# A two-layer graph network: forty rows a group fetched one by one on SyncE

## What is computed

```python
h = relu(layernorm(x))
z = (h @ W).reshape(N, 8, 16)
e = leaky_relu(el[src] + er[dst])            # el, er: z times attention vectors
a = exp(e - emax[dst])
x = x + segment_sum(z[src] * a, dst) / segment_sum(a, dst) + bias

h = relu(layernorm(x))
s, v = h[:, :32] @ W_up_s, h[:, 32:] @ W_up_v
w = silu(silu(edge_f @ A1 + b1) @ A2 + b2) @ A3
x = x + map_out(segment_sum(products(s[src], v[src], edge_y, w), dst) / 10)
```

## Time and profile before

| | us |
|---|---|
| median of 3 runs | 4053.57 |
| lowest, highest | 4052.04, 4056.43 |
| the profiled execution | 4047.16 |
| its span, first to last instruction | 4045.0 |
| GpSimd busy | 2957.0 |
| TensorE busy | 2624.4 |
| VectorE busy | 2500.3 |

### The profile page before, as it was taken

The page is one execution under the profiler, slowest core; times in us unless marked ns, Lnnn a source line. Parts: engine busy times, 40 slices in busy tenths (PEclk is TensorE's granted clock), DMA queues, the critical chain, the costliest instruction groups (busy, mean ns, idle before and its releaser), DMA issues.

```text
span 4045.0 us, 45184 instructions
## 1 busy us (share of the span) xinstructions
PE 2624.4 (65%) x11198; PEld 1908.0 (47%) x11199; DVE 2500.3 (62%) x6079; ACT 1012.2 (25%) x1447; POOL 2957.0 (73%) x3136
## 2 busy tenths in 40 slices
PE   3545555545555555545468888787887878788787
PEld 2434444444444444444445555555555555555554
DVE  7444444444444444445367777777777878777777
ACT  4333333233333233323231111111111111111111
POOL 2777777777777777777757777777777777777775
PEclk8666666666666666666679999999999999999999
DMA  4222222222222222222212222222222222222221
GB/s 126 61 60 61 60 61 60 60 60 61 61 60 61 60 61 61 61 60 62 60 44 59 57 59 59 59 60 57 58 58 60 58 60 59 59 60 59 58 59 47
DMA packets 139545, 245.74 MB, mean 61 GB/s; under 512 B 53964, under 2 KB 85814, under 8 KB 139414
## 3 DMA queue, kind: packets, MB, share of 16 engines
q0 software_dynamic: 100032, 217.87, 22.2%
q1 hardware_dynamic: 39352, 26.89, 2.4%
q10 hardware_dynamic: 144, 0.80, 0.1%
HBM read 235.32 MB, written 10.03 MB: 61 GB/s over the span
## 4 chain that ended last, share of the span: by engine, by line
POOL 44%; issue 21%; PE 16%; DVE 9%; DMA 8%; ACT 1%; DVEq 1%; POOLq 0%; ACTq 0%; SPq 0%
POOL rows L436 44%; PE pair L1299 6%; PE pair L1225 5%; DMA rows<-up_tab,idx 5%; DMA rows<-z_tab,idx 3%; DVE share L966 2%; PE pair L1256 1%; DVE share L1074 1%; DVE share L1070 1%; PE pair L1246 1%; PE pair L1250 1%; DVE acc L869 1%; DVE share L1068 1%; PE pair L1270 1%; DVE share L1079 1%
## 5 line engine op out<-in xcount | busy, mean ns | idle before, releaser
L436 POOL DMA_INDIRECT rows<-z_tab,idx x1563 | 1480.8, 947 | 547.5 <-issue 515.2
L436 POOL DMA_INDIRECT rows<-up_tab,idx x1563 | 1474.8, 944 | 518.2 <-issue 458.9
L1225 PE MATMUL pair<-share,acc 128*128 128x136 f32 x3126 | 755.5, 433 | 828.3 <-DVE share L966 828.3
L1225 PEld LDWEIGHTS pair<-share,acc 128*128 128x128 f32 x3126 | 701.2, 326 | 960.6 <-DVE share L966 958.9
L1299 PE MATMUL pair<-share,acc 128*128 128x256 f32 x3126 | 810.7, 404 | 311.1 <-DVE share L1079 309.9
L1299 PEld LDWEIGHTS pair<-share,acc 128*128 128x128 f32 x3126 | 581.5, 196 | 693.4 <-DVE share L1079 596.9
L957 DVE TENSOR_TENSOR share<-rows,share 128x64 f32<-128x64 f32 x196 | 44.5, 227 | 883.7 <-DMA rows<-z_tab,idx 883.0
L1067 DVE TENSOR_TENSOR share<-rows,pair 128x384 f32<-128x384 f32 x391 | 216.7, 554 | 343.8 <-DMA rows<-up_tab,idx 333.4
L1256 PE MATMUL pair<-weights_sb,share 128*128 128x256 f32 x1576 | 393.6, 394 | 31.3 <-ACT acc L583 31.3
L570 ACT ACTIVATE share<-pair,front_sb 128x512 f32<-128x512 f32 x198 | 136.1, 688 | 1005.1 <-PE pair L1246 1005.1
L1256 PEld LDWEIGHTS pair<-weights_sb,share 128*128 128x128 f32 x1576 | 310.2, 199 | 86.3 <-issue 40.5
(11 more groups left out here) (167 smaller groups left out, 2395.0 us busy)
## 6 DMA issues: line engine op xcount, KB each, us to landing
rows<-z_tab,idx POOLq DMA_INDIRECT x1563, 2.6
rows<-up_tab,idx POOLq DMA_INDIRECT x1563, 2.5
ef_sb<-in_edge_f SPq DMA_DIRECT2D x50, 128.0 KB, 2.7
z_tab<-rows SPq DMA_DIRECT2D x7, 504.0 KB, 3.2
y_sb<-in_edge_y SPq DMA_DIRECT2D x50, 64.0 KB, 1.8
x_sb<-in_x SPq DMA_DIRECT2D x7, 448.0 KB, 6.9
up_tab<-acc SPq DMA_DIRECT2D x49, 64.0 KB, 1.6
out<-x_sb SPq DMA_DIRECT2D x48, 64.0 KB
```

What stands on the lines that cost most here:

```text
L436: pool.indirect_dma_start(out=rows[:, s, t, 0:width], out_offset=None, in_=table, in_offset=bass.IndirectOffsetOnAxis(ap=indices[:, t:t + ...
L1225: mm = t.matmul(bank[2 + h][:, 0:MW], hot[:, s, i, :], msg[:, h, i, :], start=(i == 0), stop=(i == tiles - 1))
```

## The change

In 48 of the 49 groups, in both layers, the gather of the last column of slot 3 covers partitions 0 to 87 alone. Partitions 88 to 127 of that column are filled by SyncE with 40 plain transfers of one row each, whose source row is a register value. The indices of these edges come as an input of their own (`src_single`, 48 x 40), loaded into one partition of the memory of `dst_rel` after that is last read (`columns_set`). SyncE loads 20 of them at a time into registers. Each transfer adds 16 to one semaphore for each layer, and VectorE waits for it ahead of slot 3 (layer 1) or of its second half (layer 2). SyncE begins a group's fetch when `msg1[3]` of the group before is set, so that the place is free. In layer 1 its stores of `up_tab` now stand between the fetches, by groups; it waits until all of them have landed before the first loads of layer 2. In layer 2 the fetch stands ahead of the group's other transfers.

```diff
+SINGLE = 40
+SG = P - SINGLE
...
+            def fetch_single(tab, width, group, fetched):
+
+                for c in range(0, SINGLE, 20):
+                    _, nodes = nc.values_load_multi_w_load_instructions(
+                        single_i[0:1, bass.ds(group * SINGLE + c, 20)], engines=(mybir.EngineType.SP,), min_val=0,
+                        max_val=NODES - 1, skip_runtime_bounds_check_because="they are sources, below NODES")
+                    for i, node in enumerate(nodes):
+                        at = SG + c + i
+                        sp.dma_start(rows[at:at + 1, U - 1, T - 1, 0:width], tab[bass.ds(node, 1), 0:width])\
+                          .then_inc(fetched, 16)
+
+            sp.wait_ge(G["columns_set"], 1)
+            sp.dma_start(single_i, src_single).then_inc(loads["single"], 16)
+            sp.wait_ge(s_in["stored_early"], 16 * REUSED)
+            sp.wait_ge(s_in["stored"], 16 * (BI - REUSED))
+            sp.wait_ge(loads["single"], 16)
             sp.wait_ge(G["ready_set"], 1)
-            with sp.Fori(0, NB) as b:
-                store_up(b)
+            with sp.Fori(0, passes1) as k:
+                with sp.Fori(0, GI - 1) as q:
+                    fetch_single(z_tab, ZW, q, s_l1["single"])
+                    blocks(sp, mybir.EngineType.SP, q + 1, store_up)
+                    hold(sp, s_l1["msg1"][U - 1], k * GI + (q + 1))
+                hold(sp, s_l1["msg1"][U - 1], k * GI + GI)
+            last_blocks(sp, store_up, GI)
+            sp.wait_ge(s_mid["stored"], 16 * NB)
...
-                    blocks(sp, mybir.EngineType.SP, q, store_block)
-                    if isinstance(r, int):
-                        return
+                    if isinstance(r, int):
+                        blocks(sp, mybir.EngineType.SP, q, store_block)
+                        return
+                    fetch_single(up_tab, HIDDEN, q, s_l2["single"])
+                    blocks(sp, mybir.EngineType.SP, q, store_block)
...
             def gather(s, indices, table, width, done, n=T):
                 for t in range(n):
-                    pool.indirect_dma_start(out=rows[:, s, t, 0:width], out_offset=None, in_=table,
-                                            in_offset=bass.IndirectOffsetOnAxis(ap=indices[:, t:t + 1], axis=0))\
+                    by = slice(0, SG) if n == T and s == U - 1 and t == T - 1 else slice(0, P)
+                    pool.indirect_dma_start(out=rows[by, s, t, 0:width], out_offset=None, in_=table,
+                                            in_offset=bass.IndirectOffsetOnAxis(ap=indices[by, t:t + 1], axis=0))\
                         .then_inc(done[t // HT], 16)
...
             set_columns()
+            dve.sem_inc(G["columns_set"], 1)
...
+                            if s == U - 1:
+                                dve.wait_ge(s_l1["single"], fetched)
...
+                            if s == U - 1 and hf == 1:
+                                dve.wait_ge(s_l2["single"], fetched)
```

More of the change, by code:

```diff
@@ L64, in bc, with gnn_kernel @@
     return wide.broadcast_to(shape)
-def gnn_kernel(nc, x, src, dst, dst_lin, edge_y, edge_f, bias, front, weights, out):
+def gnn_kernel(nc, x, src, src_single, dst, dst_lin, edge_y, edge_f, bias, front, weights, out):
     with ExitStack() as ctx:
@@ L136, in gnn_kernel @@
         assert PARTS_AT + 2 * GE <= 4 * COLS and (U + 1) * GE <= COLS
-        dst_rel = sb("dst_rel", [P, NG, T])
+        early = sb("early", [P, max(NG * T, (GI - 1) * SINGLE)])
+        dst_rel = early[:, 0:NG * T].rearrange("p (g t) -> p g t", t=T)
+        single_i = early[0:1, 0:(GI - 1) * SINGLE].bitcast(I32)
         win_f = sb("win_f", [P, NG])
@@ L237, in gnn_kernel @@
         loads = {n: sem(f"load_{n}") for n in
-                 ("x0", "x1", "front", "weights", "dst", "lin", "src", "bias", "win")}
+                 ("x0", "x1", "front", "weights", "dst", "lin", "src", "single", "bias", "win")}
         zeroed = sem("zeroed")
@@ L244, in gnn_kernel @@
             "pass_set", "out_w_ready", "up_w_ready", "lin_ready",
-            "sums_cleared", "ready_set", "cleared")}
+            "sums_cleared", "ready_set", "cleared", "columns_set")}
         def named(tag, names):
@@ L263, in gnn_kernel @@
         idx_set = sem("idx_set")
-        s_l1 = named("edges", ("open", "er_sum")) | slot_sems("edges", ("spread", "square", "turned", "er", "scored", "score",
+        s_l1 = named("edges", ("open", "er_sum", "single")) | slot_sems("edges", ("spread", "square", "turned", "er", "scored", "score",
                                                          "exp", "msg0", "msg1", "agg", "added", "rows0", "rows1"))
-        s_l2 = named("l2", ("h1", "h2", "tp", "first", "weighted", "dotted")) | slot_sems("l2", ("h1_act", "h2_act")) \
+        s_l2 = named("l2", ("h1", "h2", "tp", "first", "weighted", "dotted", "single")) | slot_sems("l2", ("h1_act", "h2_act")) \
             | {n: sems(f"l2_{n}_buf", 2) for n in ("y", "ef")}
@@ L288, in blocks, with last_blocks @@
             return hi
-        def last_blocks(eng, work):
-            lo = eng.value_load(ready[0:1, GI + 1:GI + 2], min_val=0, max_val=NB - 1)
+        def last_blocks(eng, work, at=GI + 1):
+            lo = eng.value_load(ready[0:1, at:at + 1], min_val=0, max_val=NB - 1)
             with eng.Fori(lo, NB) as b:
@@ L306, in gnn_kernel @@
                    "rows1": [GI * 16 * HT] * (U - 1) + [(GI - 1) * 16 * HT]}
+        FETCHED = 16 * SINGLE
         class Own:
@@ L410, in _ @@
                 hold(sp, s_l2["h1"], (k + 1) * (NG + AHEAD))
+                hold(sp, s_l1["msg1"][U - 1], (passes1 + k + 1) * GI)
                 hold(sp, s_l1["added"][U - 1], (passes1 + k + 1) * QUADS)
@@ L938, in four_tiles @@
                     landed = dve.snap(q * (16 * HT) + 16 * HT, min_val=16 * HT, max_val=GI * 16 * HT)
+                    fetched = dve.snap((k * (GI - 1) + q + 1) * FETCHED, min_val=FETCHED, max_val=PASSES1 * GI * FETCHED)
                     _, slots = nc.values_load_multi_w_load_instructions(
@@ L1345 @@
             .reshape(NG + U, P, T).transpose(1, 0, 2)),
+        "src_single": np.ascontiguousarray(
+            laid(src, 0, extra).reshape(GI, U, P, T)[:GI - 1, U - 1, SG:, T - 1]).reshape(1, (GI - 1) * SINGLE),
         "dst": np.ascontiguousarray(
```

## The result

The changed kernel takes 4058.57 us, the median of 20 runs, against 4052.58 us of the kernel before in as many runs beside it: a ratio of 1.0016, with a 95% interval of 1.001 to 1.0023. It is 0.16% slower. I had forecast 13 us less; it came out 6 us more. The profiled execution's span is 4052.2 us, 7.1 above the 4045.0 of before; both profiled executions are short ones of their kernels (4054.28 and 4047.16 us).

A forecast was written before the change was run, and what follows sets the result against it. The prediction took the pace of GpSimd's gathers to bound both layers. From the median of 4053.57 us, -14.2 for fewer rows and +1.2 at the turn of the layers, -13.0 together, gave 4040.6 us, range 4017 to 4059.

The forecast's parts named there:

- The bound: Both layers: the pace of GpSimd's gathers, 1.25 us each, sets the time, 3906 us of the 4045.
- The price of a row on GpSimd: Last gather of slot 3: 40 rows fewer save 0.148 us a gather, 14.2 us over 96 gathers.
- (a): Rival: a gather costs an instruction, 88 rows save under 0.097 us; time 4045.5 to 4054.8 us; chance 0.22.
- the first term: GpSimd's 96 gathers of 88 rows: -14.2 us in the sum.
- the turn: Between the layers: the first feature load leaves about 1.2 us later and GpSimd stands longer, +1.2 us once.
- (c): Rival: a gather of 88 rows is slower than one of 128, by 0.1 to 0.3 us; 4064 to 4084 us; chance 0.08.
- SyncE's fetch and its cover: SyncE's 40 transfers take 21.5 us a group, the loop closes at 27, 13 us below the pace; cost 0.
- Rival (b): SyncE becomes the pace from 0.84 us a row; at 0.90, +240 us, 4294 us; chance 0.12.

The follow-up runs named there:

- the sweep: Kernel before, no fetch by SyncE, ten gathers of a group cut to 16 to 120 rows, each followed by one of 128: 4045.66 us in one run.
- the last experiment: Against the kernel with 48 gathers fewer, SyncE's wait for stored up_tab moved behind its first loads of layer 2: 3989.56 us, ratio 0.9861 to the kernel before.
- the 32 rows: Changed kernel with 32 rows a group fetched by SyncE instead of 40 and a gather of 96: 4049.43 us, ratio 1.0013 to the kernel before.

## Why the prediction was wrong

**The bound.** Right. GpSimd's pace is the clock of both layers: 48 gathers less gave 55.6 us. One reading was too smooth: of the 59.3 us before TensorE's sums, 139 times 0.30 and the stall of 9.2 make only 50.6. The rest are three stalls of 4.0, 4.0 and 1.0 us in layer 2, each right behind a stretch (10.2, 10.2 and 3.4 us long) in which TensorE's granted clock reads 0.5. They are as large after the change, in sum.

**The price of a row on GpSimd.** This is the step that failed. I had a lower bound of nought and an upper one of 0.295 us for 40 rows and took the middle, 0.148 us, though the only rows that bore on it, equal times for 576 and 512 bytes and a fixed gap, spoke for the instruction; my own list had nothing against (a). The middle of two bounds was no estimate: by the slope of the sweep 40 rows are 40 x 0.74 ns = 0.03 us, a fifth of it, and nearly half of that is taken back in the next gather (0.013 us). And for 88 rows the sign is the other one. In place of -96 x 0.148 = -14.2 us stands +96 x 0.061 = +5.9 us. That 4058.57 still lies in the stated 4017 to 4059, by 0.4 us, is luck: the upper end was made of (a) and 4 us of scatter, with no gather dearer.

The sentence of the Trainium skill that I set against the gain, in "DMA: Bandwidth & Descriptors", section "Anatomy of one DMA", that many descriptors come before their cost is seen, agrees with the 0.74 ns a row. By it the first term would have been about nought, and the sum the +1.2 us of the turn.

**Rivals (a) and (c).** The ratio is within (a)'s 0.2%, or at its edge, but the time is 3.8 us above the 4054.8 at which (a) ended. (a)'s reason, a price of the instruction, is shown by the sweep and by the whole gather taken away. But the sign is (c)'s, a short gather that takes longer than a full one, at 0.061 us with its successor where I had priced it at 0.1 to 0.3. I gave (c) 0.08 because by the Trainium skill, "DMA: Bandwidth & Descriptors", section "Why a DMA increments its semaphore by 16 and not by 1", 88 rows would go to 11 engines with eight rows each, no more than now. What the trace shows to grow is GpSimd's own time in the instruction (the landing of these gathers it doesn't show), and there the counts that this rule deals to 16 engines (16 to 112 in steps of 16) are the cheap ones and those with a smaller divisor (120: 15, 88: 11, 100 and 40: 10) the dear ones. The rule finds the families; my conclusion from it was contradicted. That the engines' number is the cause isn't shown.

**SyncE's fetch and its cover.** Right. I had estimated 0.50 us a row and 21.5 us a group; it took 0.46 and 18.5, and the price of nothing held with 16 us to spare: VectorE never waits for these rows in the changed kernel, and the fetch alone lengthens neither the last gather of a group nor the next. Rival (b), from 0.84 us a row, had no part in it.

**The turn.** The mechanism was right, the size not: +0.57 us instead of +1.2. Relative to layer 2's first gather the feature load left 1.0 us later (1.36 us ahead of it instead of 2.36), and about half of that came through, as 1.03 us gave 0.5 in the last experiment. The trace shows what hides some of the rest: TensorE's first matmul on these features began 0.85 us later (1.21 us behind that gather instead of 0.36), but its granted clock rose from 0.5 to 1.0 nearly as early (14.0 us behind it, and 13.6 before the change), so that one fewer of the radial network's matmuls (line 1256 before, 1295 after) took 631 ns instead of 379. The sums then began 0.60 us later.

**What I had not in the sum.** 1.5 us of layer 1, in the first gather of slot 3. The 1.57 us by which the first gather starts earlier are no gain of the change: over all eight traces it starts between 71.9 and 73.4 us.

## What to carry to other kernels

Where an engine issues gathers at one pace whatever their bytes, the price is the instruction's: count instructions, not rows, and move work off that engine until a whole instruction goes. Between two far bounds take the end that the nearest rows speak for, and when a kind of instruction is to run in a size that the trace doesn't show, let the price be negative too. Keep row counts of a gather a multiple of 16, and see that the queue that takes over the rows ends well before they are read.

## What the runs showed of the hardware

A gather whose row count 16 doesn't divide costs GpSimd 0.04 to 0.08 us more than the line of the others, and any gather of under 128 rows lengthens the next one, by 0.013 us in one family and 0.033 in the other. Why the next one pays is open.

A transfer of one row with its address from a register costs SyncE 0.46 to 0.49 us, loads of registers included, in runs of 40 and of 64. Between 576 and 512 bytes there is no difference to see: forty take 18.55 and 18.51 us, the medians of layers 1 and 2.

The first gather of slot 3 in layer 1 takes 0.97 us instead of 0.94 wherever SyncE fetches beside it (the changed kernel, the fetch without the shorter gather, the 32 rows). With the short gather alone it is two gathers of slot 2, columns 6 and 7, that do (0.967 and 0.957 us), though SyncE fetches nothing. So it isn't SyncE's traffic alone. Timelines of GpSimd and of VectorE in the kernel after, at the same time, and then of both in the kernel before:

```profile
1068.91 0.98 POOL L468 DMA_INDIRECT rows<-z_tab,idx  x1 [0.30 <-issue]
```

```profile
1068.78 0.29 DVE L949 TENSOR_SCALAR share<-x_sb,share 128x128 f32 x1
1069.64 0.29 DVE L951 COPY share<-pair 128x128 f32<-128x128 f32 x1 [0.57 <-PE pair L1234]
```

```profile
1068.04 0.94 POOL L436 DMA_INDIRECT rows<-z_tab,idx  x1 [0.30 <-issue]
```

```profile
1068.25 0.29 DVE L916 TENSOR_SCALAR share<-x_sb,share 128x128 f32 x1
```

It goes with VectorE's work on a finished block of targets, which the edits move against the gathers. After the change the step of line 949 begins in GpSimd's 0.30 us between two gathers, 0.13 us ahead of the longer one; before (line 916) it begins 0.21 us inside a gather. The three kernels with the fetch have both cases, 47 blocks each. In 39, 33 and 38 the step begins in the gap, 0.11 to 0.13 us ahead of a gather, and every one of those gathers takes 0.97 to 0.99 us. In the other 8, 14 and 9, and in all 47 of the kernel before, it begins inside a gather, and that one takes 0.94 or 0.95. So the longer gather goes with the place of VectorE's work against the gap, and not with the fetch, which stands in both cases. Which of the block's steps it is, and by what it acts, was not tried by itself and stays open.
